# The attention's decay rates on eight partitions, spread over the rows by transfers

## The reference

```python
x = x + 0.5 * ffn(layernorm(x))        # 8 experts, capacity 320, first-come routing
x = x + attention(layernorm(x))
x = x + 0.5 * ffn(layernorm(x))
```

```python
alpha = (sigmoid(hidden @ aW.T + ab) * 0.1).mean(-1)          # per batch and token
eta   = (sigmoid(hidden @ eW.T + eb) * 0.9 + 0.05).mean(-1)
theta = (softplus(hidden @ tW.T + tb) * LR).mean(-1)
def step(carry, xs):
    Sm = et * Sm - tt * gt                                    # momentum
    Wm = (1.0 - at) * Wm + Sm                                 # memory
for c0 in range(0, S, CHUNK):                                 # CHUNK = 128
    g = clipped gradients of |silu(k W1.T) W2.T - v|^2 at the state that the chunk begins with
    h = silu(einsum('btd,btod->bto', q, W1t))
    outs.append(einsum('bto,btpo->btp', h, W2t))
out = rmsnorm(retrieved @ Wo.T) * norm_g * (hidden @ gW.T + gb)
```

## Time and profile before

| | us |
|---|---|
| median of 3 runs | 763.94 (763.81 to 764.12) |
| the profiled execution | 763.48 |
| its span | 761.6 |
| attention, one chunk in the steady part (five stretches) | 46.0 to 46.75 |
| VectorE busy in the stretch 345.3 to 391.4 | 43.98 of 46.10 |
| TensorE busy there | 44.97 of 46.10 |
| ScalarE busy there | 33.16 |
| GpSimd busy there | 16.73 |

### The profile page before, as it was taken

One profiled execution on the slowest core, in us unless ns is written; L12 is line 12 of the kernel. 1 busy time (PEld: TensorE's weight loads), 2 busy tenths in 40 slices (PEclk: granted clock), 3 DMA queues, 4 the chain that ended last, 5 costly groups with the idle time before them and its releaser, 6 DMA issues. The chain is left out here.

```text
span 761.6 us, 15491 instructions
## 1 busy us (share of the span) xinstructions
PE 667.9 (88%) x5715; PEld 579.5 (76%) x5715; DVE 606.7 (80%) x1373; ACT 438.4 (58%) x1105; POOL 243.7 (32%) x201
## 2 busy tenths in 40 slices
PE   5449999998787889999999999999988469999996
PEld 2238989897575877988888798887967257989985
DVE  1868877862498999999999999999985869887851
ACT  1416566661466676687776777767463456557550
POOL 0033462214211434071441705325071051661302
PEclk9759999999899999999999999999999669999999
DMA  8949736340501013032130311303012814754401
GB/s 338 438 159 360 262 91 236 130 123 33 169 1 56 1 44 124 1 102 66 57 111 1 118 50 56 112 1 111 2 46 67 276 46 139 261 162 155 133 13 35
DMA packets 58226, 89.26 MB, mean 117 GB/s; under 512 B 6960, under 2 KB 49072, under 8 KB 58032
## 3 DMA queue, kind: packets, MB, share of 16 engines
q1 hardware_dynamic: 46176, 70.28, 26.5%
q0 software_dynamic: 3840, 10.49, 4.2%
q10 hardware_dynamic: 8144, 7.61, 3.2%
HBM read 74.73 MB, written 22.02 MB: 127 GB/s over the span
## 5 line engine op out<-in xcount | busy, mean ns | idle before, releaser
L726 PE MATMUL ps<-moe_normedT_high,weights_high_up 128*128 128x320 f32 x252 | 80.8, 321 | 0.6 <-DVE moe_hidden_low L544 0.5
L1240 POOL TENSOR_TENSOR att_o_rs<-att_o_mean,minus_half 128x4 f32<-128x4 f32 x16 | 16.2, 1011 | 194.6 <-DVE att_o_mean L1498 194.6
L727 PE MATMUL ps<-moe_normedT_low,weights_high_up 128*128 128x320 f32 x252 | 78.1, 310 | 0.0
L728 PE MATMUL ps<-moe_normedT_high,weights_low_up 128*128 128x320 f32 x252 | 78.1, 310 | 0.0
L726 PE MATMUL ps<-weights_high_down,moe_hidden_high 128*128 128x256 f32 x256 | 73.3, 286 | 0.0
L544 DVE SCALAR_TENSOR_TENSOR moe_hidden_low<-ps,moe_hidden_high 128x256 fp32r<-128x256 f32 x128 | 54.1, 423 | 22.7 <-ACT moe_hidden_high L681 18.6
L728 PE MATMUL ps<-weights_high_down,moe_hidden_low 128*128 128x256 f32 x256 | 71.4, 279 | 0.0
L727 PE MATMUL ps<-weights_low_down,moe_hidden_high 128*128 128x256 f32 x256 | 71.4, 279 | 0.0
L640 ACT CAST weights_high_down<-weights_raw_down 128x256 fp32r<-128x256 f32 x96 | 35.1, 407 | 39.2 <-PE ps L728 32.8
L726 PEld LDWEIGHTS ps<-weights_high_down,moe_hidden_high 128*128 128x128 f32 x256 | 48.0, 188 | 3.1 <-issue 3.1
L318 DVE TENSOR_TENSOR weights_low_down<-weights_raw_down,weights_high_down 128x256 fp32r<-128x256 f32 x128 | 50.1, 420 | 0.0
(11 more groups left out here) (328 smaller groups left out, 2068.8 us busy)
## 6 DMA issues: line engine op xcount, KB each, us to landing
weights_raw_up<-in_w SPq DMA_DIRECT2D x16, 1024.0 KB, 9.3
weights_raw_down<-in_w SPq DMA_DIRECT2D x16, 1024.0 KB, 8.6
first_xt<-in_xT SPq DMA_DIRECT2D x8, 1024.0 KB, 8.3
weights_rows<-x SPq DMA_DIRECT2D x8, 1024.0 KB, 5.5
out_x<-weights_rows SPq DMA_DIRECT2D x8, 1024.0 KB, 4.6
weights_rows<-x ACTq DMA_DIRECT2D x7, 1024.0 KB, 5.6
weights_rows<-x SPq DMA_DIRECT2D x2, 512.0 KB, 4.3
weights_raw_up<-in_w_x SPq DMA_DIRECT2D x1, 768.0 KB
```

The source lines that it names most:

```text
L726: mm(dst, high_l, high_r, start=start, stop=False)
L727: mm(dst, high_l, low_r, start=False, stop=False)
L728: return mm(dst, low_l, high_r, start=False, stop=stop)
L1240: g.tensor_tensor(o_rs[:, n], o_mean[:, n], t["minus_half"][:, n], ALU.pow).then_inc(o_rs_ready, 1)
```

## The change

1. The rates are made with the batch as partition. TensorE's `mean_rates` makes 8 products of 128 columns, one a batch, into 40 partitions of one bank (the eight momentum rates on 32 to 39, the eight keep rates on 0 to 7). ScalarE reads two pieces of 8 x 128 into `rates`.
2. SyncE stores `rates` to DRAM and loads them back onto all 128 partitions as `eta` and `keep` (512 KB each).
3. VectorE runs the decays' recurrences on 8 partitions x 128 (`decay_scans`: three scans and one copy). SyncE stores the result and loads it back as `AB` (four transfers of 64 rows x 516 values, 128 KB each). `carry_scans` is gone.
4. `second_hidden` on TensorE makes each batch's layer on its own 64 partitions only: 16 products instead of 32. ScalarE applies silu twice, to its own and to the other half: 4 operations of 64 x 512 instead of one of 128 x 1024.
5. VectorE's list is put in another order; GpSimd's too.

The core of the diff (the new `softplus` and `thetas` places and the first and last step follow the same pattern):

```diff
+            def spread_rates(c):
+                sp.wait_ge(rates_read, 2 * c + 2)
...
+                sp.dma_start(rates_dram[:, :, 1:].rearrange("i b t -> b i t"), rates[:, :, 1:]).then_inc(rates_stored, 16)
+                sp.wait_ge(rates_stored, 16 * c + 16)
+                if c:
+                    sp.wait_ge(mom_ready, c)
+                    sp.wait_ge(m_ready, c)
+                for i, dst, done in (1, eta, eta_loaded), (0, keep, keep_loaded):
+                    sp.dma_start(dst[:].rearrange("p b t -> p (b t)"), over_rows(rates_dram[i], P)).then_inc(done, 16)
+
+            def spread_decays(c):
+                sp.wait_ge(decays_made, 4 * c + 4)
...
+                sp.dma_start(decays_dram[0, :, 0:CH], decay[:]).then_inc(decays_stored, 16)
+                sp.dma_start(decays_dram[1], mixed[:]).then_inc(decays_stored, 16)
+                sp.wait_ge(decays_stored, 32 * c + 32)
+                if c:
+                    sp.wait_ge(hid2_ab_ready, c)
+                    sp.wait_ge(qab_ready, c)
+                    sp.wait_ge(mix_ready, 2 * c)
+                for n, own, other in SIDES:
+                    for i, rows in (0, own), (1, other):
+                        sp.dma_start(AB_ends[rows, n, :].rearrange("p b t -> p (b t)"), over_rows(decays_dram[i, n, :], D)
+                                     ).then_inc(ab_loaded, 16)
...
                 load_res(c + 1)
+                if c + 2 < NCH:
+                    spread_rates(c + 2)
+                    spread_decays(c + 2)
...
             def query_decay(c, very_first):
-                pool.wait_ge(ab_ready, c + 1)
+                pool.wait_ge(ab_loaded, 64 * c + 64)
...
-            def carry_scans(c, first):
...
+            def decay_scans(c):
+                dve.wait_ge(rates_read, 2 * c + 2)
+                if c:
+                    dve.wait_ge(decays_stored, 32 * c)
+                v.tensor_tensor_scan(gain[:], rates[:, 1, :], zeros[:, 0:CH], 1.0, ALU.mult, ALU.add).then_inc(decays_made, 1)
+                v.tensor_tensor_scan(decay[:], rates[:, 0, :], zeros[:, 0:CH], 1.0, ALU.mult, ALU.add).then_inc(decays_made, 1)
+                dve.wait_ge(decays_made, 4 * c + 1)
+                v.tensor_tensor_scan(mixed[:, 0:CH], rates[:, 0, :], gain[:], 0.0, ALU.mult, ALU.add).then_inc(decays_made, 1)
+                v.tensor_copy(mixed[:, CH:CH + 1], gain[:, CH - 1:CH]).then_inc(decays_made, 1)
...
+            def mean_rates(c):
+                act.wait_ge(rates_made, c + 1)
...
+                s.activation(rates[:, 1, :], A[RATE_ROWS:RATE_ROWS + B, 0, 0:CH], ACT.Copy, bias=0.5, scale=0.45
+                             ).then_inc(rates_read, 1)
+                s.activation(rates[:, 0, :], A[0:B, 0, 0:CH], ACT.Copy, bias=0.95, scale=-0.05).then_inc(rates_read, 1)
...
-                s.activation(hid2[:], wide(DD), ACT.Silu).then_inc(hid2_ready, 1)
+                for n, own, _ in SIDES:
+                    last = s.activation(hid2[own, n, :], wide(DD)[own, 0:HALF, :], ACT.Silu)
+                last.then_inc(hid2_ready, 1)
+                for n, own, other in SIDES:
+                    last = s.activation(hid2[other, n, :], wide(DD)[own, 0:HALF, :], ACT.Silu)
+                last.then_inc(hid2_doubled, 1)
...
+            def mean_rates(c):
+                pe.wait_ge(ae_sig, c + 1)
+                pe.wait_ge(kv_copied, c + 1)
+                for b in range(B):
+                    last = mm(A[0:RATE_ROWS + B, 0, 0:CH], mean[:, B - 1 - b:RATE_ROWS + 2 * B - 1 - b],
+                              sig_ae[:, b * CH:(b + 1) * CH], start=(b == 0), stop=(b == B - 1))
                 last.then_inc(rates_made, 1)
```

More of the change, by code:

```diff
@@ L973 @@
 WX = 7 * D + H + D
+RATE_ROWS = 32
 class AttentionInputs:
@@ L1171, in _ @@
                     sp.sem_clear(s)
+            for c in range(2):
+                spread_rates(c)
+                spread_decays(c)
             for c in range(NCH - 1):
@@ L1261, in step @@
                     mix(c + 1, False)
+                output_power(c, 0)
+                if not last:
                     residual(c, par, 0)
@@ L1265, in step @@
                     return
+                if c + 2 < NCH:
+                    hidden(c + 1, 1 - par, False)
                 residual(c, par, 1)
@@ L1285, in start @@
             def start():
-                v.memset(lead[:], 0.0).then_inc(folded, 1)
-                v.memset(eta[:, :, 0:1], 0.0)
-                v.memset(keep[:, :, 0:1], 0.0).then_inc(folded, 1)
+                v.memset(zeros[:], 0.0).then_inc(cleared, 1)
                 v.memset(spare[:], 0.0).then_inc(lg_read, 1)
@@ L1339, in tap, with key_taps @@
                 last.then_inc(done, 1)
-            def convolve_keys(c, par):
-                for n in range(1, TAPS):
+            def key_taps(c, par, taps):
+                for n in taps:
                     tap(c, (KV[par], raw_kv, conv_kv, kv_conv), n)
+                if taps.stop < TAPS:
+                    return
                 dve.wait_ge(kv_conv, TAPS * c + TAPS)
@@ L1394, in memory_scans @@
                 v.tensor_tensor_scan(run(M[:]), run(keep[:]), run(mom[:]), 0.0, ALU.mult, ALU.add).then_inc(m_ready, 1)
-            def decay_scans(c, first):
-                dve.wait_ge(carry_ready, c + 1)
-                if not first:
-                    dve.wait_ge(qab_ready, c)
-                v.tensor_tensor_scan(run(AB[:]), run(keep[:]), run(carry[:]), 0.0, ALU.mult,
-                                     ALU.add).then_inc(ab_ready, 1)
             def ends(c, par, first):
@@ L1535, in last_step @@
                 slope_of(c)
+                softplus(c, par)
                 output_mean(c - 1, 1)
@@ L2043, in second_hidden @@
                     pe.wait_ge(x2_turned_copied, 2 * c)
-                for b in range(B):
-                    for rows in (slice(0, D), slice(D, P)):
-                        mm(wide(DD)[rows, b, :], state[par][:, b, D:2 * D], QAB[:, b, :], start=True, stop=False)
-                    for rows in (slice(0, D), slice(D, P)):
-                        last = mm(wide(DD)[rows, b, :], grad_w1[:, b, :], P1[:, b, :], start=False, stop=True)
+                for i in range(HALF):
+                    for n, own, _ in SIDES:
+                        b = n.start + i
+                        mm(wide(DD)[own, i, :], state[par][:, b, D:2 * D], QAB[:, b, :], start=True, stop=False)
+                    for n, own, _ in SIDES:
+                        b = n.start + i
+                        last = mm(wide(DD)[own, i, :], grad_w1[:, b, :], P1[:, b, :], start=False, stop=True)
                 last.then_inc(pre2_made, 1)
```

187 lines of the change are left out of this document (88 added, 99 removed).

## The result

The changed kernel takes 767.15 us (median of 5 runs, 765.58 to 768.27) against 763.94 (5 runs, 763.70 to 764.22): ratio 1.0045, 95% interval 1.0033 to 1.0056. It is slower by 3.2 us; 757.4 was forecast. The profiled execution took 766.61 with a span of 764.5 (before: 763.48 and 761.6).

The account below looks back on a forecast made before the run. Two nearly equal loops between TensorE and VectorE were taken as the bound, so the steady step stays 46.1 us. Start -5.8, step 1 -1.1, last step +0.4 sum to -6.5: 763.94 to 757.4, range 751.5 to 765.5.

Parts of the forecast that it names:

- Turn of x to the rates' products: Steady loop, first stretch on TensorE, from `turn_x` to the rates' products: 16.25 us, with nothing in it changed.
- the wait ahead of `retrieve`: Steady chunk: TensorE's savings, 1.8 from `second_hidden` and 0.6 from earlier gradients, become a wait of about 2.7 us.
- From there to `turn_x` TensorE is dense, 12.73 in both.: Steady loop, last stretch, from `retrieve` to `turn_x`: TensorE takes 12.73 us before and after the change.
- the start: Start of the attention: `AB` of chunk 0 is loaded long before, so `turn_x` of chunk 2 comes at 273.7, -5.8 us.
- the loop: Steady chunk through rates, short scans, convolution, second scores, `retrieve` and `turn_x`: 46.1 us, unchanged.
- the forecast's own case: Whole kernel: a time of 755 to 760 us, given a chance of 0.50.
- case 1: Steady loop shorter, as taps run under other waits: 0.8 us in each of six steps, 752.5 us; chance 0.14.
- Case 4: `eta` lands late behind a 1 MB load, 2.5 us seven times: slower, 775 us; chance 0.10.
- Case 3: The start gives nothing, chunk 0's `eta` and `keep` come late, the preamble waits 5: 762.5 us; chance 0.09.
- Case 2: VectorE is the bound and its 4.6 - 1.2 counts, six times 3.4 us: 737 us; chance 0.04.
- Case 5: GpSimd's norm power starts just ahead of the short scans, blocks them 1.3 us in five steps: 764; chance 0.08.
- Case 6: GpSimd's decayed queries block the momentum scan, 2.3 us in six steps: 771 us; chance 0.05.

Follow-up runs that it names:

- The kernel with the old layer: Changed kernel with the second layer back at 32 products and one silu, rates, transfers and GpSimd's order kept as changed: 758.92 us, ratio 0.9958.
- GpSimd's order undone: Changed kernel with GpSimd's decayed queries and mix back behind the first power of the output norm: 767.0 us, ratio 1.0066.
- the taps moved: Changed kernel with VectorE's key taps 2 and 3 moved behind the memory scan and its ends, except in the first step: 765.29 us, ratio 1.0023.
- those four kernels: Changed kernel with key taps moved: alone 765.29 us; with GpSimd's order undone too 743.26; that with only tap 3 moved 748.06; with the old layer 755.61.
- the best version: Changed kernel with key taps 2 and 3 behind the memory scan and GpSimd's queries and mix behind the first output-norm power: 743.26 us, ratio 0.9760.

## Why the prediction was wrong

- **Turn of x to the rates' products**, 16.25: measured 385.01 - 368.76 = 16.25. Right, as were the rates and the read (2.42 predicted, 2.57 to the first short scan), the short scans (1.2; measured 1.02), the convolution to the scores (13.5; 13.60) and the wait ahead of `retrieve` (2.7; 2.45). VectorE waits 1.07 for the rates, not 0.2; it was sooner there than reckoned, which costs nothing.
- **"From there to `turn_x` TensorE is dense, 12.73 in both."** This is the step that failed. It is dense, but TensorE's durations were taken from a trace in which no wait stood ahead of it, at a granted clock of 1.00. Behind the new wait of 2.45 a part of it ran at the lower level: 14.33. Five times 1.6 is 8.0 us; filling the wait (wholly or by four products) or taking it away brought the ratio from 1.0045 to 0.9962, 0.9952 and 0.9958, which is 6.3 to 7.1 us. I had let TensorE's freed 2.4 us "become a wait" at no cost, without asking what the wait does to the work behind it, and no rival had it. The kernel before had a hint that I did not take up: it already puts `unread_products` (L2185), products that nobody reads, into TensorE's waits in the start and the last step of the attention.
- **Without the clock**, the loop is 46.30 (46.1 predicted), the start gives -5.25 (-5.8), the first step -0.6 (-1.1). With +0.6 in the four steps, +0.6 in the last one and -0.6 behind it, the time would be 763.9 - 5.2 = 758.7, within the 755 to 760 of the forecast's own case. The kernel with the old layer has a median of 758.9; by its ratio it would be 0.9958 x 763.94 = 760.7, just above that. So most of the miss is the clock, and what is left against 757.4 is 1.3 to 3.3 us.
- **The start's -5.25 is near the forecast by two errors that offset each other.** The preamble was put at 0.8 later and is 0.1 later (`turn_x` of chunk 1 at 232.85 for 232.77), and the second scores end at 261.49, 1.0 before the 262.5 forecast. From there to `turn_x` it takes 12.8, not 11.2. Some of that is GpSimd: its decayed queries (262.64) meet the memory scan, which takes 3.51, and `retrieve` to `turn_x` is 12.25; with GpSimd's order undone these are 2.28 and 11.42.
- **The range** is said to reach down to case 1, with 751.5; case 1's own sum is 752.5. Nothing hangs on it.
- **Transfers**: `eta` is never a releaser in the changed kernel. It is issued at 392.54, takes 3.9 (median) and is wanted at 398.80: 2.4 of margin against 2.1. Case 4 did not come. With the taps moved the scan comes earlier, and in three of those four kernels `eta` was late once: 0.68, 1.06 and 0.15.
- **Case 3** fell with the start's 5.25. **Case 1**: no step is under 46.3. **Case 2** in the changed kernel is wrong (VectorE has waits), but its sense, that work ahead of the scores decides, is what the best version used.
- **Case 5**: the order came, the blocking did not. The norm's power ran at 249.65 for 1.64 and the short scan at 249.78 took 0.41; in the steady step the power runs from 386.59 to 388.23 and the short scan at 387.58 takes 0.41 too. That is its usual time (0.40 at 220.30, with no power beside it).
- **Case 6**: the decayed queries began 1.6 to 3.7 us behind the start of the momentum scan, which kept its 2.28 in all six of these chunks, and met the memory scan instead; in the steady part that cost nothing by itself. In the start they held VectorE up ahead of the gradients, as predicted, but in the operation ahead of the factor: 1.72 for 0.28.

```profile
241.51 2.18 POOL L1245 TENSOR_TENSOR weights_raw_up<-weights_raw_up,att_AB 128x1024 f32<-128x1024 f32 x1
```
```profile
242.00 1.72 DVE L1475 TENSOR_SCALAR att_THETA<-att_theta_sum 128x8 f32<-128x8 f32 x1
```

## What to carry to other kernels

Work taken from TensorE in front of a point that another engine releases becomes a wait, and in this kernel a wait of 2.45 us cost 1.6 more behind it by the clock, one of 1.5 nothing. Before counting such a wait as free, ask what runs behind it on TensorE, and price the products right behind the wait by rows at the lower level (0.71 for 0.42 here). Shorten the other engine's way to that point first: the same shorter layer cost 6.6 us without that and gained 11.4 with it. Filling the wait only took the loss back: 0.9962 and 0.9952, against 0.9958 with the old layer.

## What the runs showed of the hardware

- A wait of TensorE that is short against the step can be enough for the lower level: `retrieve`'s products took 0.71 for 0.42 us behind 2.45, the turn of the keys 1.94 for 1.03 behind 2.44. It need not be: behind a wait of 2.44 in the start the clock held in seven kernels of ten. Products whose results nobody reads hold the clock as real ones do (1.00 behind all twelve waits with four or nine of them).
- A VectorE copy of four values per partition takes 1.98 us beside a GpSimd product of two 128 x 1024 operands, and the memory scan 3.99 for 2.28 beside that product and the mix behind it, while the short scan beside a GpSimd power on 128 x 8 keeps its 0.41. The Trainium skill (SBUF — State Buffer, "Who interferes with whom") says that a VectorE instruction with two SBUF inputs contends with a GpSimd instruction that reads SBUF; the memory scan agrees with it, the short scan, which also has two, does not.
